# Pacing the gathers of a four-pass graph kernel: seven side sums behind TensorE in place of ten, and in the third pass the product of the gather's own step

## The chip, the cores and the metric

The kernel runs on one core of one Trainium2 chip. The metric is the device time of one execution in microseconds (us); the time that is compared is the median of several executions. Engines are named as in the profile: PE is TensorE, PEld its weight loads, DVE VectorE, ACT ScalarE, POOL GpSimd, SP SyncE. A small q behind a name means the engine's sequencer.

## The reference

Four graph layers over 12,500 nodes of 128 numbers and 200,000 edges that are sorted by their target node. Each layer gathers a source row per edge, scores the edge, takes a softmax over the edges of each target and sums the weighted rows. Layer 0 holds two such passes (its `gatv2_layer` twice), layer 1 is computed by source (a scatter pass), layer 2 has a score that is the sum of one number of the target and one of the source, and layer 3 has eight heads:

```
xj = xl[src];  e = leaky_relu(xj + xr[dst]);  logits = e @ att          # layer 0, twice; layer 3 with 8 heads
score = logit[dst] + logit_src[src]                                    # layer 2: no vector per edge
m = segment_max(logits, dst);  ex = exp(logits - m[dst])
out = segment_sum(ex * xj, dst) / segment_sum(ex, dst)
```

## The kernel before, in words

The edges lie in 1664 steps of 128 (one edge a partition). Sixteen steps make a turn, four steps a chunk, so a pass has 104 turns of four chunks. The function family `sp_edges`, `pool_edges`, `pe_edges`, `act_edges`, `dve_edges` runs one pass, each on its own engine, and is called four times: E0 and E1 (layer 0, source tables gather_a and gather_b), E2 (layer 2, table gather_s, `vector` is False) and E3 (layer 3, table gather_c, eight heads, `wide`). Between E1 and E2 lies a pass of another kind (scatter, lines 1151 to 1340) that the change does not touch. Text below calls E0, E1, E2, E3 the first, second, third and fourth pass.

In one turn, per step g:

- SP loads the turn's tables (L665 to L669), once the sums of the turn four before are all added.
- POOL issues one indirect DMA for each step (L687): it gathers 128 source rows into `rows[:, turn mod 4, g]`. Ahead of it stands a wait, `hold_ge`, on PE's semaphore `side_sums`: ten side sums back. It is a wait for pace alone; that the slot in `rows` is free is told by the wait on `block_sums` four turns back (L684).
- PE makes the side sum of the step (L721 and L722): target row of each edge by a one-hot matmul, plus the gathered source row by a matmul with the identity. For a chunk it waits for the four gathers of that chunk (L711) and for DVE's `larger` two chunks back. In the third pass the side sum is only the target's score (L725, a 128x4 result): it reads no gathered row, and PE does not wait for gathers there.
- ACT and DVE turn the side sums into logits (L862, L908, L915, L921). In the third pass DVE adds the target's score and the source's score once a turn (L1095 to L1103) and waits there for all sixteen gathers of its turn.
- Two turns later PE makes the block sums (L738) from weighted one-hots of ACT (L826) and the gathered rows, and DVE adds them to the totals (L951, L960).
- A chain of small PE transposes (L774, L779, L782, L789, L792) and DVE scans carries the running maxima from turn to turn; DVE's `rescale` (L978) waits for L792, ACT's L826 for the edge distances of PE (L747).

Each engine takes its instructions strictly in program order. `side_sums` is counted by PE as each side sum is finished; `L.side.at(it, k, lag=1)` is side sum k of the turn before.

Of the kernel before, what the change touches and what calls it, by code (L numbers as in the profile page):

```python
# [16 lines left out]
G = 16  # L17
# [1 line left out]
PEEL = 2 * U  # L19
CH = 4  # L20
NCH = G // CH
LEAD = 10
AW = 136
XW = 130
NSUM = 4
# [135 lines left out]
def turns(eng, n, depth, turn, ahead=0):  # L161


    assert ahead <= U
    end = n - U if ahead else n
    for i in range(PEEL):
        turn(Turn(i))
    with eng.Fori(PEEL // U, end // U) as j:
        for u in range(U):
            turn(Turn(u, j))  # L170
    for i in range(end, n + depth):
        turn(Turn(i))


def build(nc, a, out):
# [31 lines left out]
    with ExitStack() as ctx:  # L207
# [468 lines left out]
        def pool_edges(e, L):  # L676
            w = On(e, anchor)
            w.wait_ge(L.opened.at(0))

            def turn(it):  # L680
                u = it.slot()
                w.hold_ge(L.tab.at(it))
                for c in range(NCH):
                    w.hold_ge(L.block.at(it, c, lag=U))  # L684
                    for g in range(c * CH, (c + 1) * CH):
                        w.hold_ge(L.side.at(it, g - LEAD) if g >= LEAD else L.side.at(it, g + G - LEAD, lag=1))
                        e.indirect_dma_start(rows[:, u, g, 0:L.width], None, L.src_rows,  # L687
                                             bass.IndirectOffsetOnAxis(ap=edge_sb[:, u, g:g + 1].bitcast(I32), axis=0)
                                             ).then_inc(L.gat[c].sem(it), 16)
            turns(e, NG, 0, turn)  # L690
# [1786 lines left out]
```

## Time and profile before

| | |
|---|---|
| median of 3 runs | 14911.71 us (14908.64 to 14938.14) |
| the profiled execution, own time | 14998.32 us |
| its span in the trace | 14996.4 us |
| mean granted clock of PE | 0.72 of full speed |
| PE, DVE, ACT, POOL busy | 74%, 53%, 37%, 63% of the span |

Busy shares are averages over stages with different limits. POOL's share counts the time in which it makes a gather's descriptors, not the transfer; what ends an idle stretch is inferred from semaphore events, and "remote" there means that no engine's instruction was found close to the event. "issue" means that nothing in the profile was waited for.

### The profile page before, as it was taken

To read this page: it belongs to the slowest core of one execution; us is meant where nothing else is said; L and a number is where in the kernel's file an instruction comes from. 1 tells how busy PE (TensorE), PEld (TensorE's weight loads), DVE (VectorE), ACT (ScalarE), POOL (GpSimd) and SP (SyncE) were. 2 spreads that over 40 slices of the span, in tenths; PEclk is the share of its full clock that TensorE was granted. 3 is DMA by queue.
4 is the path that set the end of the run, shared out by engine and by line. 5 is a ranking of instruction groups with operands and counts; after the bars stand their busy time and mean duration, and the time that the engine had idled before them with its cause. 6 is when DMAs were issued, how large, how long until landed. Compare 5 with 4: busy or idle time off the path is not lost.

```text
span 14996.4 us, 278163 instructions
## 1 busy us (share of the span) xinstructions
PE 11026.0 (74%) x60653; PEld 8678.6 (58%) x60653; DVE 7973.5 (53%) x29240; ACT 5541.4 (37%) x14105; POOL 9489.8 (63%) x8593
## 2 busy tenths in 40 slices
PE   5777777777777778888888875555555767777776
PEld 4666666666666666666666653344344556666664
DVE  6555555555555555555555553333333566666666
ACT  1444444344444444333333343333333622222223
POOL 3666666466666657888888865566666255655555
PEclk7887788788778775766666765555555877888777
DMA  3111111221111113444444452222222221222222
GB/s 87 45 45 44 44 45 45 88 80 44 45 44 45 44 40 44 39 39 39 39 39 39 39 104 58 44 45 45 45 45 45 60 52 48 50 49 49 50 50 56
DMA packets 808955, 748.01 MB, mean 50 GB/s; under 512 B 264685, under 2 KB 691174, under 8 KB 808254
## 3 DMA queue, kind: packets, MB, share of 16 engines
q0 software_dynamic: 453440, 550.05, 21.1%
q1 hardware_dynamic: 354814, 191.38, 4.9%
q14 instruction: 599, 4.91, 0.1%
q8 instruction: 102, 1.67, 0.0%
HBM read 548.62 MB, written 192.13 MB: 49 GB/s over the span
## 4 chain that ended last, share of the span: by engine, by line
PE 27%; another core or an unknown queue 15%; issue 13%; DMA 9%; DVE 7%; ACT 6%; POOL 2%; SPq 1%; DVEq 1%; ACTq 0%; POOLq 0%
DMA scatter_s<-dst_side 8%; PE bank L738 8%; PE bank L721 3%; PE bank L722 3%; PE bank L1214 3%; ACT oh_e L826 2%; PE bank L1220 2%; PE bank L1229 2%; PE bank L747 2%; PE bank L705 1%; POOL scatter_s L1181 1%; DVE agg L960 1%; DVE lrelu L915 1%; DVE agg L951 1%
## 5 line engine op out<-in xcount | busy, mean ns | idle before, releaser
L738 PE MATMUL bank<-rows,oh_e 128*128 128x130 f32 x9984 | 2172.6, 376 | 1578.7 <-ACT oh_e L826 1172.1
L1181 POOL DMA_INDIRECT scatter_s<-dst_side x1664 | 2568.6, 1544 | 551.9 <-DMA scatter_s<-dst_side 267.1
L738 PEld LDWEIGHTS bank<-rows,oh_e 128*128 128x128 f32 x9984 | 1804.0, 264 | 1918.7 <-issue 1036.4
L826 ACT ACTIVATE oh_e<-bank,weight,minus_w 128x128 f32<-128x128 f32 x4992 | 1880.3, 459 | 2378.4 <-remote 1620.8
L951 DVE SCALAR_TENSOR_TENSOR agg<-agg,rescale,bank 128x130 f32 x4992 | 1683.4, 337 | 1636.6 <-remote 792.6
L722 PE MATMUL bank<-rows,ident 128*128 128x128 f32 x9984 | 2335.9, 319 | 144.8 <-issue 141.1
L687 POOL DMA_INDIRECT rows<-gather_c,edge_sb x1664 | 1650.9, 992 | 1122.4 <-issue 443.9
L687 POOL DMA_INDIRECT rows<-gather_b,edge_sb x1664 | 1672.5, 1005 | 1061.9 <-issue 423.0
L687 POOL DMA_INDIRECT rows<-gather_a,edge_sb x1664 | 1669.1, 1003 | 1008.5 <-issue 412.0
L687 POOL DMA_INDIRECT rows<-gather_s,edge_sb x1664 | 1574.3, 946 | 1061.2 <-issue 443.2
L722 PEld LDWEIGHTS bank<-rows,ident 128*128 128x128 f32 x9984 | 1894.7, 235 | 159.7 <-issue 157.6
L862 ACT ACTIVATE lrelu<-bank 128x512 f32<-128x512 f32 x1248 | 751.2, 602 | 2734.9 <-PE bank L722 1900.8
L721 PE MATMUL bank<-dst_side,oh_t 128*128 x4992 | 1253.8, 338 | 202.5 <-issue 116.5
L721 PE MATMUL bank<-dst_side,hT 128*128 x4992 | 1232.0, 334 | 96.9 <-issue 93.2
L908 DVE TENSOR_TENSOR lrelu<-lrelu,bank 128x512 f32<-128x512 f32 x1248 | 850.5, 681 | 714.4 <-ACT lrelu L862 520.0
L705 PE MATMUL bank<-oh_rows,oh_w 5*128 5x512 bf16 x1664 | 788.6, 474 | 556.5 <-ACT oh_t L811 290.5
L721 PEld LDWEIGHTS bank<-dst_side,oh_t 128*128 128x128 f32 x4992 | 950.9, 236 | 311.4 <-issue 280.7
L721 PEld LDWEIGHTS bank<-dst_side,hT 128*128 128x128 f32 x4992 | 932.2, 232 | 194.5 <-issue 153.8
L1214 PE MATMUL bank<-rows,dst_side 128*128 128x130 f32 x3328 | 775.0, 399 | 343.1 <-DVE dst_side L1290 325.8
L1299 DVE SCALAR_TENSOR_TENSOR dst_side<-iota,edge_sb,bank 128x98 f32<-128x98 f32 x1664 | 432.4, 315 | 1115.9 <-PE bank L1220 1078.3
L738 PE MATMUL bank<-xw,oh_e 128*128 128x136 f32 x3328 | 620.4, 339 | 510.5 <-DVE xw L931 218.2
L1214 PEld LDWEIGHTS bank<-rows,dst_side 128*128 128x128 f32 x3328 | 653.2, 278 | 577.0 <-DVE dst_side L1290 359.6
(352 smaller groups left out, 18169.2 us busy)
## 6 DMA issues: line engine op xcount, KB each, us to landing
rows<-gather_a,edge_sb POOLq DMA_INDIRECT x1664
rows<-gather_b,edge_sb POOLq DMA_INDIRECT x1664
scatter_s<-dst_side POOLq DMA_INDIRECT x1664
rows<-gather_s,edge_sb POOLq DMA_INDIRECT x1664
rows<-gather_c,edge_sb POOLq DMA_INDIRECT x1664
rows<-scatter_s SPq DMA_DIRECT2D x56, 455.0 KB, 6.3
scatter_s<-zeros SPq DMA_DIRECT2D x64, 390.0 KB
edge_sb<-edge_tab SPq DMA_DIRECT2D x520, 40.0 KB
```

What stands on the lines that cost most here:

```text
L687: e.indirect_dma_start(rows[:, u, g, 0:L.width], None, L.src_rows, bass.IndirectOffsetOnAxis(ap=edge_sb[:, u, g:g + 1].bitcast(I32), axis= ...
L705: e.matmul(bank[0][:, :], oh_w[:, :], oh_rows[:, it.slot(lag), c * CH * P:(c + 1) * CH * P], start=True, stop=True).then_inc(L.dist.sem, 1)
L721: e.matmul(o, oh, dst_flat[:, bass.ds(at[g], P)], start=True, stop=False)
L722: e.matmul(o, ident[:, :], rows[:, it.slot(), g, 0:P], start=False, stop=True).then_inc(L.side.sem, 1)
L738: ins = e.matmul(sum_bank(g)[:, (g % 2) * AW:(g % 2) * AW + L.aw], oh_e[:, g % 8, :], r, start=True, stop=True)
L826: e.activation(oh_e[:, g % 8, :], bank[7][:, (g % CH) * P:(g % CH + 1) * P], ACT.Relu, bias=weight[:, it.slot(2, 2), g:g + 1], scale=minus ...
L862: e.mul(lrelu[:, c % 2, :], bank[2 + c % 2][:, :], SLOPE).then_inc(L.sloped.sem, 1)
L908: e.tensor_tensor(lrelu[:, c % 2, :], lrelu[:, c % 2, :], bank[2 + c % 2][:, :], ALU.max).then_inc(L.larger.sem, 1)
L951: e.scalar_tensor_tensor(old, old, rescale[:, it.slot(2, 2), g:g + 1], sum_bank(g)[:, (g % 2) * AW:(g % 2) * AW + L.aw], ALU.mult, ALU.add ...
L1181: e.indirect_dma_start(scatter_s[k], bass.IndirectOffsetOnAxis(ap=S_.target[:, it.slot(1), g:g + 1], axis=0), S_.summed[:, g % 8, :], None ...
L1214: e.matmul(bank[6 + h % 2][:, (g % 2) * XW:(g % 2 + 1) * XW], S_.same[:, g % 8, :], rows[:, v, g, :], start=True, stop=True).then_inc(S_.b ...
L1299: e.scalar_tensor_tensor(S_.scratch[:, g % CH, 0:NB], iota[:, 0:NB], edge_sb[:, u, 4 * G + g:4 * G + g + 1], bank[5][:, (g % CH) * P:(g % ...
```

## The change

The number of side sums that a gather stays behind goes from ten to seven. In the third pass (`L.vector` False) each gather waits for the product of its own turn and step. Nothing else is touched: same instructions, same buffers.

```diff
-LEAD = 10
+LEAD = 7
@@ pool_edges @@
                     for g in range(c * CH, (c + 1) * CH):
-                        w.hold_ge(L.side.at(it, g - LEAD) if g >= LEAD else L.side.at(it, g + G - LEAD, lag=1))
+                        if L.vector:
+                            w.hold_ge(L.side.at(it, g - LEAD) if g >= LEAD else L.side.at(it, g + G - LEAD, lag=1))
+                        else:
+                            w.hold_ge(L.side.at(it, g))
                         e.indirect_dma_start(rows[:, u, g, 0:L.width], None, L.src_rows,
```

On POOL's queue the difference shows where a pass starts, before the wait has a side sum to wait for. The start of the first pass before and after, in POOL's order (side_sums is the semaphore of PE's side sums, x9 that the row stands nine times):

```order
L687 DMA rows<-gather_a,edge_sb 128x128 [waits tables_in_slot0,rows_and_carry_set]
L687 DMA rows<-gather_a,edge_sb 128x128 x9
L687 DMA rows<-gather_a,edge_sb 128x128 [waits side_sums] x6
L687 DMA rows<-gather_a,edge_sb 128x128 [waits side_sums,tables_in_slot1]
L687 DMA rows<-gather_a,edge_sb 128x128 [waits side_sums] x15
```

```order
L690 DMA rows<-gather_a,edge_sb 128x128 [waits tables_in_slot0,rows_and_carry_set]
L690 DMA rows<-gather_a,edge_sb 128x128 x6
L690 DMA rows<-gather_a,edge_sb 128x128 [waits side_sums] x9
L690 DMA rows<-gather_a,edge_sb 128x128 [waits side_sums,tables_in_slot1]
L690 DMA rows<-gather_a,edge_sb 128x128 [waits side_sums] x15
```

Seven gathers go without a wait where ten did; every later gather has moved by three side sums. The start of the third pass on POOL, before and after:

```order
L687 DMA rows<-gather_s,edge_sb 128x129 [waits tables_in_slot0,rows_and_carry_set]
L687 DMA rows<-gather_s,edge_sb 128x129 x9
L687 DMA rows<-gather_s,edge_sb 128x129 [waits side_sums] x6
L687 DMA rows<-gather_s,edge_sb 128x129 [waits side_sums,tables_in_slot1]
L687 DMA rows<-gather_s,edge_sb 128x129 [waits side_sums] x15
```

```order
L690 DMA rows<-gather_s,edge_sb 128x129 [waits side_sums,tables_in_slot0,rows_and_carry_set]
L690 DMA rows<-gather_s,edge_sb 128x129 [waits side_sums] x15
L690 DMA rows<-gather_s,edge_sb 128x129 [waits side_sums,tables_in_slot1]
L690 DMA rows<-gather_s,edge_sb 128x129 [waits side_sums] x15
L690 DMA rows<-gather_s,edge_sb 128x129 [waits side_sums,tables_in_slot2]
```

No gather of the third pass goes without a wait now; each has moved by ten side sums.

## Rows read from the trace of the kernel before

**Rows 1.** The page: the span, and the gathers of the four passes (busy, mean ns, idle)

```profile
span 14996.4 us, 278163 instructions
...
L687 POOL DMA_INDIRECT rows<-gather_c,edge_sb x1664 | 1650.9, 992 | 1122.4 <-issue 443.9
L687 POOL DMA_INDIRECT rows<-gather_b,edge_sb x1664 | 1672.5, 1005 | 1061.9 <-issue 423.0
L687 POOL DMA_INDIRECT rows<-gather_a,edge_sb x1664 | 1669.1, 1003 | 1008.5 <-issue 412.0
L687 POOL DMA_INDIRECT rows<-gather_s,edge_sb x1664 | 1574.3, 946 | 1061.2 <-issue 443.2
```

**Rows 2.** Line 687: ns min/median/max, first to last start; then idle us, times

```profile
L687 POOL DMA_INDIRECT rows<-gather_a,edge_sb x1664: 941/947/1763, 220.7 to 2849.4; - x185
L687 POOL DMA_INDIRECT rows<-gather_b,edge_sb x1664: 941/947/1764, 2952.7 to 5583.7; - x185
L687 POOL DMA_INDIRECT rows<-gather_s,edge_sb x1664: 941/947/1068, 9091.1 to 11698.1; - x185
L687 POOL DMA_INDIRECT rows<-gather_c,edge_sb x1664: 941/947/1796, 12026.2 to 14779.1; - x185
...
  PE bank L722: 1075.5, 687
  remote: 979.3, 536
  PE bank L725: 216.1, 120
```

**Rows 3.** Timeline in the first pass: start, us, engine, line, [idle before]

```profile
1501.86 0.63 PE L722 MATMUL bank<-rows,ident 128*128 128x128 f32 x2
...
1503.28 0.94 POOL L687 DMA_INDIRECT rows<-gather_a,edge_sb  x1 [1.93 <-PE bank L722]
...
1509.90 0.95 POOL L687 DMA_INDIRECT rows<-gather_a,edge_sb  x1 [1.92 <-PE bank L722]
...
1511.72 0.39 PE L722 MATMUL bank<-rows,ident 128*128 128x128 f32 x2
...
1513.65 0.94 POOL L687 DMA_INDIRECT rows<-gather_a,edge_sb  x1 [0.30 <-issue]
...
1515.90 0.60 ACT L862 ACTIVATE lrelu<-bank 128x512 f32<-128x512 f32 x1 [2.38 <-remote]
...
1516.43 0.95 POOL L687 DMA_INDIRECT rows<-gather_a,edge_sb  x1 [1.84 <-PE bank L722]
```

**Rows 4.** Timeline in the third pass

```profile
10001.61 0.95 POOL L687 DMA_INDIRECT rows<-gather_s,edge_sb  x1 [1.79 <-PE bank L725]
...
10007.41 0.17 DVE L1103 TENSOR_TENSOR masked<-logit,edge_sb 128x16 f32<-128x16 f32 x1
...
10011.40 0.28 PE L792 MATMUL bank<-ident,decay_m 16*128 16x16 f32 x1
...
10017.35 0.95 POOL L687 DMA_INDIRECT rows<-gather_s,edge_sb  x1 [0.30 <-issue]
...
10019.21 0.17 DVE L978 TENSOR_SCALAR rescale<-bank 128x16 f32<-128x16 f32 x1 [11.63 <-remote]
```

**Rows 5.** Timeline at the start of the first pass: fourth gather, first side sum

```profile
224.46 0.95 POOL L687 DMA_INDIRECT rows<-gather_a,edge_sb  x1 [0.30 <-issue]
...
227.26 0.79 PE L721 MATMUL bank<-dst_side,oh_t 128*128 x2 [5.23 <-DMA rows<-gather_a,edge_sb]
```

**Rows 6.** Line 721: what PE waited for at it, us and times

```profile
  DMA rows<-gather_c,edge_sb: 36.6, 23
  DMA rows<-gather_b,edge_sb: 16.9, 7
...
  DMA rows<-gather_a,edge_sb: 15.0, 8
```

**Rows 7.** Stretches of the first and third pass: length; busy of PE, PEld, DVE, ACT, POOL; PEclk, DMA share, GB/s

```profile
230.00:2830.00 2600.00, 2010.33 (x12312) 1642.75 (x12311) 1413.53 (x4257) 1072.26 (x2733) 1647.32 (x1643) 0.81 0.18 45
...
9100.00:11690.00 2590.00, 1396.89 (x7401) 1014.23 (x7401) 835.45 (x3354) 861.60 (x2329) 1561.78 (x1651) 0.50 0.21 46
```

## The prediction, made before the changed kernel ran

> **What bounds the kernel now.** The page comes first. Each pass has 1664 gathers [rows 1], and by the view of line 687 the passes run from 220.7 to 2849.4, 2952.7 to 5583.7, 9091.1 to 11698.1 and 12026.2 to 14779.1 us [rows 2]. Over 104 turns that is 25.3, 25.3, 25.1 and 26.5 us a turn. The reader should see how alike these are, though PE is 77% busy in the first pass (2010.33 of 2600 us) and 54% in the third (1396.89 of 2590) at different clocks [rows 7]. What the passes share is POOL: one gather keeps it 1.003 us on average, the next one starts 0.30 us behind it at the earliest [rows 1, 3], so sixteen take 16 x 1.303 = 20.8 us in the first pass, 16 x 1.246 = 19.9 us in the third and 16 x 1.292 = 20.7 us in the fourth. The rest, 4.4, 5.2 and 5.8 us a turn, is time in which POOL waits for side sums. It is in pieces: 687 + 536 + 120 waits of 1075.5 + 979.3 + 216.1 us [rows 2], 3.2 a turn over 416 turns, 1.7 us each or 1.4 us above the 0.30.
>
> The timeline says why a piece is never short. In the first pass a chunk's side sums start to be ready at about 1512.1 (the pair of matmuls that began at 1511.72 took 0.39 us), yet ACT, which needs that chunk, starts at 1515.90, and POOL, which waits for its first sum, at 1516.43 [rows 3]. Between them lies the last gather of a row of four, begun at 1513.65. ACT moved 2.25 us after that start, POOL 2.8 us. The first chunk shown had its first sum finished at 1502.49 while POOL stood still, and POOL went on at 1503.28, 0.8 us later [rows 3]. In the third pass PE is through L792 at 10011.68, DVE's L978, which needs it, starts at 10019.21, 1.9 us after the last of a row of gathers had begun at 10017.35 [rows 4]. So I read: while gathers follow each other without a break, PE's finished work is often not seen by the others until about 2 us after the start of the last gather. A wait of POOL costs 1.9 us (1.93, 1.92 and 1.84) and is also what lets the other engines go on.
>
> Here the Trainium skill speaks against that reading. Its page "SBUF — State Buffer", section "SBUF: two separate sides", says that transfers and engines use disjoint ports and cannot slow each other. The 7.5 us of L978 are not explained by it; by the page alone the distance of the gathers would be mere slack and the sum below would be zero.
>
> **The change, part by part.** No instruction is added: 4 x 1664 gathers keep their 0.95 us and their wait; only the number waited for differs. At the start of the passes fewer gathers go ahead: three less in the first, second and fourth, hidden because PE needs four at first and seven are still free; ten less in the third, once 10 x 1.25 = 12 us at most. I count 12 us.
>
> First, second and fourth pass. After side sum 4c has been seen, gather 4c+7 may start, and it is the last one that the next chunk of side sums needs; before, the fourth gather of a chunk had been released three side sums earlier. The loop from chunk to chunk is: sum seen to gather start 0.8 us [rows 3]; start to landing as PE sees it 2.8 us (224.46 to 227.26) [rows 5]; first sum of the chunk 0.7 to 1.2 us (L721 and L722 pairs, 0.39 to 0.79 us each) [rows 3, 5]. Together at most 4.8 us, less than the 4 x 1.303 = 5.2 us that POOL needs for the four gathers. Two ends follow:
> - every completion is seen at once: POOL never waits, a turn falls to 20.8 us, 4.4 us below today;
> - every chunk's sums are held back until the row of four gathers is over: four waits a turn of 1.93 - 0.30 = 1.63 us, 6.5 us, a turn of 27.3 us, 2.1 us above today.
> Between the ends counts the share h of chunks that are held back: 6.5h against 4.4 us now, so the border is h = 0.68. Now PE can have the sums of two chunks done inside one row of gathers, since its gathers have landed long before (it waited 38 times for one, 68 us in three passes [rows 6]), and one wait then frees eight gathers; with seven it can't. The new first sum of a chunk is finished 2.8 + 0.7 us or more after POOL has gone on. A completion in that position is the one of 1512.1, 2.2 us after POOL went on at 1509.90, and it was held [rows 3]; the one of 1502.49 was free, but POOL stood still there. I take h = 0.8: 5.2 us a turn, +0.8 us. In the fourth pass the waits take 1.4 us more than in the first today (5.8 against 4.4); I leave these and add the same 0.8 us. Behind a waiting gather stand only POOL's other gathers; who waits for them is PE, at the side sums, and behind these in PE's order its block sums, transposes and edge distances.
>
> Third pass. PE's products need no gathered row, so POOL's rhythm stays as it is and only the labels of the gathers move by ten. New is that DVE at L1095 waits for gathers that have just been issued. With chunks two and three released together at about 10001.6, eight gathers start from there on, the last 7 x 1.25 = 8.8 us later at 10010.4, landed at 10013.2 by the 2.8 us of rows 5. L1095 to L1103 take 0.9 us, so the masked scores come at 10014.1 and not at 10007.6. PE transposes them early, but what it hands on is seen at 10019.2 anyway [rows 4]: 5 us of cover, cost nothing. Where a row of gathers ends early the cover is gone and up to 6.5 us would show. I take 0.3 us a turn between 0 and 1.
>
> Sum: 104 x (0.8 + 0.8 + 0.8 + 0.3) + 12 = 293 us. The profiled execution took 14998.32 us for a span of 14996.4 us, 0.6% above the median of the runs shown; I add the 293 us to the median, 14911.71, and get 15,200 us.
>
> **The rivals.**
> - Faster: shorter rows of gathers let completions through. The loop of 4.8 us fits into 5.2 us, and with at most seven ahead the engines behind PE are never cut off as long as in rows 4. It decides from h = 0.68 down. For it speaks that the free loop would take POOL out of its waits altogether; against it the held sum of 1512.1. With h = 0.5 a turn of the three passes is 3.25 - 4.4 = 1.15 us shorter: 3 x 104 x 1.15 = 359 us less, 43 us more for the third pass and the start: 14,600 us.
> - Every chunk is held back (h = 1): 104 x (3 x 2.1 + 0.3) + 12 = 698 us more, 15,610 us. For it: the position of the new first sum late in the row. Against it: some completions do pass.
> - No change: PE's finished work is late for a reason that has nothing to do with how far ahead the gathers are, and the slack of seven is enough, as 38 waits for landings in 312 turns suggest. 14,900 us. The page's rule above would give this.
> - The clock. PE waits more and stays at 1.2 GHz. In the third pass, at 54% busy, the granted clock is 0.50, in the first 0.81 [rows 7]. At 0.50 the 19.5 us of PE in a turn of the first pass would become 31.7 us, above the 25.3 us, and the three passes would lose 6 us a turn, 1900 us: 16,800 us. A PE that is the bound is busy, and it was at 0.81 when busy 77%, so I hold this for improbable. The Trainium skill, "TensorE: Matmul & The Clock Gate", section "HAM oscillation — how this bites in real kernels", describes waits for transfers that bring the clock down; the trace agrees in so far as the pass with the less busy PE has 0.50.
>
> **How the numbers follow.** A measurement of this kernel tells about 0.2% (30 us) from no change. Chances: slower by the partial hold-up 0.42 (15,050 to 15,500 us), every chunk held 0.06, clock 0.02; no change 0.13; faster 0.37 (14,350 to 14,850 us). Slower together 0.50. The range goes from h = 0.43 (2.8 - 4.4 = 1.6 us a turn less in three passes, -456 us: 14,450) to h = 1 (15,600); about 0.1 is left out below and 0.06 above. The forecast's own range, without the faster case, is 15,050 to 15,600.
>
> **What the changed profile would show.** If right: POOL's waits for PE L722 more in number, near four a turn, still 1.8 to 1.9 us each, few rows of gathers longer than four; PE waiting for rows<-gather at L721 hundreds of times in place of 38; turns of 26 us in the first two passes; the third pass at 25 us a turn with DVE waiting at L1095 for rows<-gather_s. If the rival is right: fewer or shorter waits of POOL, the turn below 25 us, and in the third pass L978 no longer 7 us behind L792. The prediction is wrong if the share of held-back chunks falls with shorter rows of gathers, or if the order of the third pass, where DVE now waits, changes which completions meet a row of gathers.

## The result and the profile after

| | us | ratio to before (95% interval) |
|---|---|---|
| before, median of 6 | 14907.83 | |
| changed, median of 6 | 14976.85 | 1.0041 (1.0030 to 1.0053) |
| changed, profiled execution: span | 14967.4 | |

The kernel became 0.41% slower (the ratio), some 62 us; the two medians lie 69 us apart. The forecast was 15,200 us, some 290 us slower.

The page of the changed kernel, the rows that answer to [rows 1]:

```profile
span 14967.4 us, 278163 instructions
...
L690 POOL DMA_INDIRECT rows<-gather_c,edge_sb x1664 | 1661.3, 998 | 1075.2 <-PE bank L725 501.3
L690 POOL DMA_INDIRECT rows<-gather_b,edge_sb x1664 | 1660.6, 998 | 1060.9 <-PE bank L725 444.0
L690 POOL DMA_INDIRECT rows<-gather_a,edge_sb x1664 | 1661.3, 998 | 997.8 <-PE bank L725 416.8
L690 POOL DMA_INDIRECT rows<-gather_s,edge_sb x1664 | 1574.5, 946 | 1105.5 <-issue 448.7
```

The view of its gather line, as [rows 2] (L690 is L687 of before; L725 and L728 are L722 and L725):

```profile
L690 POOL DMA_INDIRECT rows<-gather_a,edge_sb x1664: 942/947/1764, 220.4 to 2830.3; - x185
L690 POOL DMA_INDIRECT rows<-gather_b,edge_sb x1664: 942/947/1761, 2932.4 to 5551.8; - x185
L690 POOL DMA_INDIRECT rows<-gather_s,edge_sb x1664: 942/947/1083, 9064.1 to 11712.2; - x185
L690 POOL DMA_INDIRECT rows<-gather_c,edge_sb x1664: 942/947/1800, 12033.7 to 14750.2; - x185
...
  PE bank L725: 1362.2, 893
  remote: 599.2, 367
  PE bank L728: 341.9, 122
```

The waits rose from 1343 to 1382, but the mean wait fell from 1.69 to 1.67 us. The spans of the two first profiles mislead: before's own is 0.6% above its median, so the changed kernel looks faster there. They can't be subtracted; hence a second profile of before, below.

What PE waited for at line 724, as [rows 6], and DVE at line 1098 (L1095 of before), which waited there once, for 7.9 us:

```profile
  DMA rows<-gather_c,edge_sb: 199.0, 134
  DMA rows<-gather_b,edge_sb: 69.8, 39
  DMA rows<-gather_a,edge_sb: 46.4, 23
```

```profile
L1098 DVE TENSOR_REDUCE logit<-bank x104: 219/225/226, 9085.6 to 11717.2; 128x16 f32<-128x64 f32 x104
its engine sat idle before it (us, times) until:
  DMA rows<-gather_s,edge_sb: 124.2, 38
```

PE now waits 196 times for a landing in place of 38, 315 us in place of 68, and DVE 38 times, 3.3 us each. Both are as the forecast described them, in kind. For PE these named waits are the smaller part: the row "issue" of the same view, idle time for which the profile names no cause, rose from 644.2 to 1913.4 us. The timeline of the changed kernel in the first pass:

```profile
1515.07 0.95 POOL L690 DMA_INDIRECT rows<-gather_a,edge_sb  x1 [0.30 <-issue]
...
1515.33 0.39 PE L725 MATMUL bank<-rows,ident 128*128 128x128 f32 x2
...
1518.32 0.94 POOL L690 DMA_INDIRECT rows<-gather_a,edge_sb  x1 [2.31 <-PE bank L725]
...
1518.90 0.61 ACT L865 ACTIVATE lrelu<-bank 128x512 f32<-128x512 f32 x1
```

The pair that holds the first sum is over at 1515.72, yet POOL goes on 2.6 us later, 3.25 us after the last gather of the row began. The delay that the forecast was built on is there.

Of the signs that the forecast named, some are there and some are not. Landings at line 724 are waited for hundreds of times. But POOL waits 3.3 times a turn (1382 over 416 turns) and not near four, the first two passes take 25.1 and 25.2 us a turn and not 26, and the third 25.5.

### The profile page after: what moved, and what is told of

Its sections match the earlier page's. It is cut to its first block, busy times and chain, and to the rows that moved or that the text cites. A ratio compares the mean times of both kernels' runs of the same rounds, so it can differ in the third digit from the quotient of the medians.

```text
span 14967.4 us, 278163 instructions
## 1 busy us (share of the span) xinstructions
PE 11047.6 (74%) x60653; PEld 8764.4 (59%) x60653; DVE 7967.3 (53%) x29240; ACT 5571.8 (37%) x14105; POOL 9480.8 (63%) x8593
## 3 DMA queue, kind: packets, MB, share of 16 engines
q8 instruction: 102, 1.67, 0.0%
## 4 chain that ended last, share of the span: by engine, by line
PE 31%; another core or an unknown queue 14%; issue 11%; DMA 8%; DVE 8%; ACT 5%; POOL 2%; DVEq 1%; ACTq 0%; POOLq 0%; SPq 0%
PE bank L741 7%; DMA scatter_s<-dst_side 6%; PE bank L724 4%; PE bank L725 4%; PE bank L1217 3%; PE bank L1223 2%; ACT oh_e L829 2%; PE bank L1232 2%; PE bank L750 2%; PE bank L708 1%; DVE agg L963 1%; DVE lrelu L918 1%; POOL scatter_s L1184 1%; DMA rows<-gather_c,edge_sb 1%
## 5 line engine op out<-in xcount | busy, mean ns | idle before, releaser
L741 PE MATMUL bank<-rows,oh_e 128*128 128x130 f32 x9984 | 2076.0, 364 | 1006.0 <-ACT oh_e L829 615.5
L741 PEld LDWEIGHTS bank<-rows,oh_e 128*128 128x128 f32 x9984 | 1734.6, 256 | 1335.1 <-issue 681.9
L725 PE MATMUL bank<-rows,ident 128*128 128x128 f32 x9984 | 2424.2, 333 | 1.1 <-issue 0.7
L690 POOL DMA_INDIRECT rows<-gather_c,edge_sb x1664 | 1661.3, 998 | 1075.2 <-PE bank L725 501.3
L690 POOL DMA_INDIRECT rows<-gather_b,edge_sb x1664 | 1660.6, 998 | 1060.9 <-PE bank L725 444.0
L690 POOL DMA_INDIRECT rows<-gather_a,edge_sb x1664 | 1661.3, 998 | 997.8 <-PE bank L725 416.8
L690 POOL DMA_INDIRECT rows<-gather_s,edge_sb x1664 | 1574.5, 946 | 1105.5 <-issue 448.7
L725 PEld LDWEIGHTS bank<-rows,ident 128*128 128x128 f32 x9984 | 2005.5, 249 | 2.0 <-issue 1.9
L724 PE MATMUL bank<-dst_side,oh_t 128*128 x4992 | 1319.8, 356 | 522.9 <-issue 306.7
L724 PE MATMUL bank<-dst_side,hT 128*128 x4992 | 1265.0, 343 | 526.2 <-issue 386.9
L724 PEld LDWEIGHTS bank<-dst_side,oh_t 128*128 128x128 f32 x4992 | 1017.1, 253 | 627.8 <-issue 614.2
L724 PEld LDWEIGHTS bank<-dst_side,hT 128*128 128x128 f32 x4992 | 969.2, 241 | 625.3 <-issue 605.6
L1071 DVE TENSOR_TENSOR shifted<-masked,bank 128x16 f32<-128x16 f32 (+1 forms) x416 | 83.3, 200 | 1654.3 <-remote 1170.5
```

Source lines behind the costliest of these rows:

```text
L724: e.matmul(o, oh, dst_flat[:, bass.ds(at[g], P)], start=True, stop=False)
L725: e.matmul(o, ident[:, :], rows[:, it.slot(), g, 0:P], start=False, stop=True).then_inc(L.side.sem, 1)
L741: ins = e.matmul(sum_bank(g)[:, (g % 2) * AW:(g % 2) * AW + L.aw], oh_e[:, g % 8, :], r, start=True, stop=True)
```

## The experiments

All runs are compared with the kernel before, run beside them on the same chip. That matters here. The 18 runs were made in five groups, and before took 14909, 14979 and 14983 us in three of the groups and 12863 and 12864 us in the two others. I call these the first and the second kind of chip. It was not chosen which one a group got, and whether the chip or something around it differs is not known: the record gives a number for the chip, and number 9 stands both with a group of the second kind (e4 to e7) and with one of the first kind (e8 to e10).

| run | back, vector passes / third | kind | ratio (95% interval) |
|---|---|---|---|
| e0_before | 10 / 10 | first | 1.0003 (0.9993 to 1.0013) |
| e1_vector7 | 7 / 10 | first | 1.0033 (1.0022 to 1.0044) |
| e2_third_own | 10 / own step | first | 1.0015 (1.0006 to 1.0024) |
| e8_after_again, e15_after | 7 / own step | first | 1.0047 (1.0033 to 1.0062), 1.0044 (1.0030 to 1.0058) |
| e3_vector4_third7 | 4 / 7 | first | 1.1809 (1.1793 to 1.1826) |
| e17_lead13 | 13 / 13 | first | 1.0320 (1.0298 to 1.0341) |
| e10_no_pace_again | no wait | first | 1.2186 (1.2166 to 1.2207) |
| e9_break | 10 / 10, break after each gather | first | 1.2374 (1.2354 to 1.2393) |
| e16_break_no_pace | no wait, break after each fourth | first | 1.0585 (1.0524 to 1.0646) |
| e4_lead13, e11_lead13_again | 13 / 13 | second | 1.0005 (0.9996 to 1.0014), 1.0001 (0.9991 to 1.0010) |
| e5_no_pace | no wait | second | 0.9996 (0.9987 to 1.0005) |
| e6_pad | 10 / 10, six idle waits after each gather | second | 1.0009 (1.0000 to 1.0018) |
| e7_third7 | 10 / 7 | second | 1.0005 (0.9996 to 1.0014) |
| e14_vector6 | 6 / 10 | second | 1.0610 (1.0592 to 1.0628) |
| e12_break_no_pace | no wait, break after each fourth | second | 1.1184 (1.1165 to 1.1203) |
| e13_chunk_break | 10 / 10, break after each fourth | second | 1.1412 (1.1393 to 1.1432) |

### The change in its two parts

e0_before is the kernel before, unedited. The others change only the numbers:

```diff
-w.hold_ge(L.side.at(it, g - LEAD) if g >= LEAD else L.side.at(it, g + G - LEAD, lag=1))
+if L.vector:   # e1: 7, e2: 10, e3: 4
+    w.hold_ge(L.side.at(it, g - 7) if g >= 7 else L.side.at(it, g + G - 7, lag=1))
+else:          # e1: 10, e2: L.side.at(it, g), e3: 7
+    w.hold_ge(L.side.at(it, g - 10) if g >= 10 else L.side.at(it, g + G - 10, lag=1))
```

> The kernel before, unchanged, for a second profile of it. Its first profile took 14998 us where its runs have a median of 14908, and the changed kernel's profile took 14969 us where its runs have a median of 14977; so the lengths of the passes in those two profiles can't be set against each other yet. Ratio 1.000. If the excess of 90 us in the first profile was chance, the four passes are here shorter together by some 90 us: I expect it in the three passes with vectors (2629, 2631 and 2753 us there), since POOL's pauses are the part of a turn that is not fixed. If it sits outside the four passes, the pass lengths of the first profile can be used as they are.

> Only the first part of the change: seven back in the first, second and fourth pass, ten back in the third. Theory of the prediction (completions of PE are held back while gathers follow each other; share h of chunks held): the measured 62 us of the whole change, less what the third pass costs (2648 against 2607 us in the two profiles, 41 us), leave some 20 us for three passes, h about 0.69: ratio 1.001 to 1.002. Rival (what the two profiles say as they are: 19, 12 and 36 us less in the three passes): ratio 0.996. Second rival (all the loss is here, the third pass is neutral as the prediction had it): 1.004.

> Only the second part: ten back in the first, second and fourth pass, the product of the own step in the third. By the profiles +41 us, ratio 1.0028. By the prediction (0.3 us a turn and 12 us at the start) +43 us, 1.003: the two agree, so this run can only speak against both. Rival (the third pass carries more than the whole loss, the other passes gain): +60 to +130 us, 1.004 to 1.009, and the pass by itself more than 2660 us long.

> Four back in the first, second and fourth pass, seven back in the third. With four, gather 4c+4 waits for the first sum of chunk c, so the next chunk's gathers start only when this chunk's sums are seen: the loop of a chunk is 0.8 us + three gathers 3.9 us + landing 2.8 us + first sum 0.7 to 1.2 us = 8.2 to 8.7 us, four times a turn is 33 to 35 us, each of the three passes some 800 us longer: ratio about 1.16. If landings and first sum are faster than these rows say, 1.10. Third pass at seven: theory that only the labels of the gathers move there: within 10 us of the pass of before (2607 us). Rival (shorter rows of gathers let completions through): shorter by 50 us or more.

The second profile of before:

```profile
L687 POOL DMA_INDIRECT rows<-gather_a,edge_sb x1664: 938/944/1762, 221.1 to 2818.7; - x185
L687 POOL DMA_INDIRECT rows<-gather_b,edge_sb x1664: 938/944/1764, 2920.8 to 5514.2; - x185
L687 POOL DMA_INDIRECT rows<-gather_s,edge_sb x1664: 938/944/1067, 9021.7 to 11659.3; - x185
L687 POOL DMA_INDIRECT rows<-gather_c,edge_sb x1664: 938/944/1823, 11987.9 to 14719.0; - x185
```

The passes are 2598, 2593, 2638 and 2731 us long, against 2629, 2631, 2607 and 2753 us in [rows 2]: three shorter, as expected, and the third longer. So one profile of this kernel gives the length of a pass only to about 30 us. Only the timed ratios can carry a difference of 60 us, and they do: the first part costs 0.33% (49 us), the second 0.15% (22 us), together 71 us beside the 62 us of the whole. Of the rivals for e1 the gain falls. The other, that all of the loss is in this part (1.004), lies inside the interval of e1 (1.0022 to 1.0044); what speaks against it is e2, whose interval (1.0006 to 1.0024) leaves out 1. The main expectation for e1, 1.001 to 1.002, was too low, and the 1.0028 for e2 too high. e3 hit the first pass: four back makes 33.8 us a turn (3510.6 us for 104), 8.4 us a chunk where 8.2 to 8.7 had been put together from rows, and the second and fourth pass are 3535 and 3563 us long. The ratio 1.18 is above the 1.16 expected, since the turns before were 24.9 to 26.3 us long in these passes and the loss is nearer 900 than 800 us a pass. Its third pass, seven back, took 2606 us, within the expected 10 us of 2607; but at ten back three profiles have 2607, 2638 and 2615 us, so this says little.

### Is PE's finished work held back?

> The wait for a side sum is taken out of the gathers altogether; a gather is held only by its buffer (block sums of the turn four before). If PE's completions are held back while gathers follow each other, rows of sixteen gathers and more appear, the other engines stand meanwhile, and the turn is sixteen gathers (20.8 us) and then the work that was cut off: over 28 us a turn, ratio 1.08 or more. Rival (nothing is held back, the pace is idle time of POOL that something else sets): the pauses move to the wait for the block sums and the turn stays at 25 us, ratio 0.99 to 1.01.

> The kernel before with six waits on a semaphore that was reached long ago behind each gather, so that POOL's queue has a short break after each of them in place of 0.30 us; all other waits as before. I expect 0.3 to 0.4 us more between gathers, 16 x 1.6 = 25.5 us a turn without any pause. Theory of held completions, if a break of 0.7 us is enough to let them through: POOL's long pauses all but vanish, L978 is no longer seven us behind L792 in the third pass, turn 25.5 to 26 us, ratio 1.00 to 1.03. If only a break of about 2 us after a gather lets them through: the pauses stay and the padding is added, 16 x 0.35 = 5.6 us a turn, ratio 1.14. Rival (the turn is set by a loop that has nothing to do with POOL): the padding disappears in the pauses, ratio 1.00, with PE, DVE and ACT idle as before.

> Thirteen side sums back in all four passes (buffers allow up to sixteen). Theory of held completions: rows of gathers grow, fewer waits but longer ones, and engines behind PE are cut off longer; with ten a pass has 2.6 waits of over 1 us a turn and 4.3 us of pause a turn, with seven 2.8 and 4.4 us. If the sum of pauses is what the other engines need, it stays: within 0.3 us a turn, ratio 0.993 to 1.007. Rival (POOL's pauses are a cost of waiting closely): each three sums further back save as much as from seven to ten, 0.33%: ratio 0.997 or less.

> Ten back in the first, second and fourth pass, seven in the third. In the run with four in the vector passes and seven in the third the third pass was 2606 us long; with ten it was 2607, 2638 and 2615 us in three profiles, with the own step 2647 and 2648 us. If only labels move there, ratio 1.000 (within 0.001). If the own step's cost is that DVE waits for gathers just issued, seven lies between ten and own step (zero), near ten: 1.000 to 1.0005. Rival (a gain of 15 us or more by seven): 0.999 or less.

These four fell on the second kind of chip. In none of them did the time move by more than 0.2%, and the reason stands in their profiles. Line 690 of e7_third7, whose vector passes are those of before, and its first and third pass in busy times (columns as in [rows 7]):

```profile
L690 POOL DMA_INDIRECT rows<-gather_a,edge_sb x1664: 940/944/1757, 217.6 to 2335.6; - x185
...
L690 POOL DMA_INDIRECT rows<-gather_s,edge_sb x1664: 940/944/1096, 8081.8 to 10159.2; - x185
...
  issue: 1428.8, 4684
  PE bank L725: 538.5, 1766
```

```profile
230.00:2330.00 2100.00, 1698.98 (x12392) 1414.67 (x12391) 1417.85 (x4289) 1110.21 (x2755) 1597.54 (x1649) 0.94 0.22 55
9300.00:9700.00 400.00, 279.23 (x1460) 201.79 (x1460) 164.02 (x660) 169.38 (x460) 302.46 (x321) 0.50 0.26 57
```

The third pass takes 2077.4 us for 1663 steps from gather to gather, 1.249 us each: POOL never stops, and the 1766 waits for PE (of all four passes) are 0.30 us each, which is the gap between any two gathers. The turn is 20.0 us, what the forecast had as the floor of this pass (19.9). Here POOL is the bound and the distance to the side sums is free; the granted clock in the first pass is 0.94 in place of 0.81. On this kind the forecast's second end ("every completion is seen at once") is simply the case, at ten back as well. e6_pad broke no row: its gathers kept their 0.30 us, so the six waits added nothing between them. What it was meant to show it could not.

The no-wait kernel and a real break behind each gather were then run on the first kind:

```diff
+pad = sb("pad", [P, 64]);  self.breaks = each("gather_breaks")
 ...).then_inc(L.gat[c].sem(it), 16)
+e.memset(pad[:, :], 0.0).then_inc(L.breaks.sem, 1)
+w.hold_ge(L.breaks.at(it, g))
```

> The changed kernel once more. The kernel before took 14909 us beside the runs with seven and four back and 12863 us beside the runs with thirteen back and with no pace: two chips of different behaviour. In the profiles of the second there is no pause of POOL at all (every gather 0.30 us behind the one before, 20.0 us a turn in the third pass), so on such a chip the distance can't matter: ratio 0.999 to 1.002, of which 12 us at the start of the third pass would be 0.0009. On a chip as the first one: 1.0041 again, between 1.003 and 1.005.

> The kernel before (ten back), and behind each gather a small memset of POOL for whose end POOL waits, so that the next gather can't start 0.30 us behind; the six waits of the padded run were hidden in the gather before (its gathers kept 0.30 us), so that run broke no row. I expect about 0.3 to 0.5 us more between gathers. On a chip without pauses: 16 x 0.4 = 6.4 us a turn on top of 20.0 to 20.9, four passes 2400 us longer less what PE's own time (19.5 us busy) leaves, ratio 1.15 to 1.22. On a chip as the first one, theory (PE's completions are held while gathers follow within 0.3 us, and pass when there is a real break): the long pauses vanish, turn 16 x 1.65 = 26.4 us against 25.1, ratio 1.02 to 1.05. If a longer silence is needed: pauses stay and the breaks are added, ratio over 1.12.

> No wait for a side sum at all, once more. On a chip without pauses the same as before (0.9996 there). On a chip as the first one, theory of held completions: rows of gathers run on until a buffer is missing, the engines behind PE are cut off for whole rows: ratio 1.03 or more, with fewer and much longer pauses of POOL and many slow steps of SP's sequencer. Rival (the sum of the pauses is set by something else, for example by what PE needs, and only moves from wait to wait): 0.995 to 1.01.

The same kernel without pace is 0.9996 on one kind and 1.2186 on the other. Its timeline on the first kind, first pass:

```profile
1502.21 1.17 PE L737 MATMUL bank<-rows,oh_e 128*128 128x130 f32 x8
1502.69 0.33 DVE L950 SCALAR_TENSOR_TENSOR agg<-agg,rescale,bank 128x130 f32 x1
...
1507.83 0.39 PE L720 MATMUL bank<-dst_side,hT 128*128 x2 [0.93 <-issue]
...
1509.95 0.37 PE L721 MATMUL bank<-rows,ident 128*128 128x128 f32 x1 [1.62 <-issue]
...
1512.08 0.60 PE L721 MATMUL bank<-rows,ident 128*128 128x128 f32 x2 [1.32 <-issue]
...
1512.83 0.60 ACT L861 ACTIVATE lrelu<-bank 128x512 f32<-128x512 f32 x1 [9.99 <-PE bank L721]
...
1516.71 0.94 POOL L686 DMA_INDIRECT rows<-gather_a,edge_sb  x1 [0.30 <-issue]
1520.84 0.35 DVE L950 SCALAR_TENSOR_TENSOR agg<-agg,rescale,bank 128x130 f32 x1 [17.82 <-remote]
...
1531.88 1.03 POOL L686 DMA_INDIRECT rows<-gather_a,edge_sb  x1 [14.23 <-DMA step_sb<-step_tab]
```

Gathers run on without a gap until 1516.71. DVE stands for 17.82 us, though the block sums that it needs were over at 1503.38; then everything behind PE moves within 11 us while POOL stands for 14.23 us. Two things are seen here. The word of PE's finished work comes late (DVE), and PE itself is slow: the four side sums of one chunk, between which the program has no wait, take from 1503.65 to 1512.68, with gaps of up to 1.62 us for which the profile names no cause. ACT's 9.99 us are of this second sort, since PE's last side sum was over only 0.15 us before. Over the first pass such gaps of more than 0.3 us inside a chunk's side sums come to 310 us (370 of them) without the wait, to 72 and 48 us in the two profiles of before, to 0.4 us in the changed kernel and to none in e5, e7 and e9. I counted them from the kept traces.

The hand-over from PE to DVE that took 7.5 us in [rows 4] can be quick. At one place in the third pass of e9_break, where POOL stands, and on the second kind at one where the gathers follow without a gap (e7_third7):

```profile
11505.40 0.28 PE L796 MATMUL bank<-ident,decay_m 16*128 16x16 f32 x1
11506.05 0.17 DVE L982 TENSOR_SCALAR rescale<-bank 128x16 f32<-128x16 f32 x1 [1.09 <-PE bank L796]
```

```profile
9303.48 0.94 POOL L690 DMA_INDIRECT rows<-gather_s,edge_sb  x1 [0.30 <-issue]
9303.80 0.28 PE L795 MATMUL bank<-ident,decay_m 16*128 16x16 f32 x1
9304.45 0.17 DVE L981 TENSOR_SCALAR rescale<-bank 128x16 f32<-128x16 f32 x1 [1.10 <-PE bank L795]
```

It is 0.37 us from the end of the matmul to DVE in both. Single places prove little, so here is the same wait of DVE over the third pass, from the view of its line: 909 us for 101 of them in the first profile of before and 370 us for 101 in the second; 163 us for 102 in e9_break, on the first kind but with breaks; 130 us for 102 in e5 and e7, on the second kind.

The kept traces hold one thing more that bears on the whole pass: the times at which each semaphore was raised. Beside the end of each side sum of the first pass (its first and last turns left out) I set the first raising of `side_sums` that is not more than 0.06 us earlier. A raising that belongs to the side sum before can be taken for it, so the lateness is put rather too low. Between 0.3% and 12% of the raisings are missing from a trace, so differences of a few per cent say nothing.

| run | back | kind | raised over 0.5 us late | over 1.5 us late | median, us |
|---|---|---|---|---|---|
| e3_vector4_third7 | 4 | first | 5% | 4% | 0.01 |
| e1_vector7, changed kernel, e8, e15 | 7 | first | 59% to 62% | 32% to 36% | 0.87 to 0.93 |
| before, e0_before, e2_third_own | 10 | first | 62% to 65% | 39% to 46% | 1.04 to 1.27 |
| e17_lead13 | 13 | first | 66% | 50% | 1.52 |
| e10_no_pace_again | none | first | 42% | 29% | 0.01 |
| e16_break_no_pace | none, break after each fourth | first | 56% | 32% | 0.69 |
| e9_break | 10, break after each | first | 7% | 3% | 0.01 |
| all eight of the second kind | 6, 10, 13, none | second | at most 1.2% | at most 1% | 0.01 |

In [rows 3] the four side sums that end between 1512.11 and 1513.45 are raised in one burst between 1515.66 and 1515.88; ACT starts at 1515.90 and POOL's next gather at 1516.43. So it is shown that on the first kind the others get word of PE's work late when gathers follow each other within 0.3 us, and that it comes in time when there is a break after every gather (0.88 to 1.2 us between them in the timeline), or on the second kind. It is not DVE alone that is held: in [rows 3] it is ACT and POOL. What the lateness costs by itself is not shown. The 22% of the no-wait kernel are made of both, of it and of PE's own gaps.

The break was dearer than expected: gathers follow each other at 2.0 us in the timeline and at 2.1 to 2.2 us on the average of a pass, in place of 1.25. So e9_break is slower, 1.24 against the 1.02 to 1.05 expected. By its number it lies with the other branch (over 1.12, "a longer silence is needed"), but the table speaks against the reason given there: the raisings are in time.

### Where the loss per step back lies

> Six back in the first, second and fourth pass, ten in the third. Loop of a chunk with six back: sum seen to gather start 0.8 us, one more gather 1.3, landing 2.8, first sum 0.7 to 1.2: 5.6 to 6.1 us, four times 22.4 to 24.4 us, below the turn of 25.2: by the loop alone the same as seven back, 1.003. If the pause after each row adds to the loop (a completion is seen only when the row is over), four pauses a turn of 1.63 us on 20.8: 27.3 us, three passes 2.1 us a turn more, 1.044. What comes out between them is the share of chunks that are held. (By the same loop four back was 8.2 to 8.7 us; measured 33.8 us a turn, 8.4 a chunk.)

> No wait for side sums; in its place a small memset behind every fourth gather, for whose end POOL waits, 1.05 us between two gathers there in place of 0.30 (as in the run with a break behind each gather). Theory: a break of this length is enough for PE's completions to pass, so rows are never longer than four (4.0 us of gathers and a break): 16 x 1.303 + 4 x 0.75 = 23.8 us a turn in the first pass against 25.0 to 25.3, ratio 0.94 to 0.98 if no other pause is left, against 1.2186 without breaks. Rival (the others need POOL to wait for them, a blind break helps only by chance): 1.05 or more. On the other kind of chip (before at 12860 us) the breaks only cost: 3 us a turn less what PE takes anyway, 1.04 to 1.09.

> Breaks as in e12, and the pace of ten back kept. Theory: as e12 but with what is left of the pauses of POOL added where it runs ahead: 0.95 to 0.99, L978 close behind L792 in the third pass. If breaks and pauses add up (4 x 0.75 = 3.0 us a turn, four passes): 1.08. On the other kind of chip: 1.04 to 1.09.

> Thirteen side sums back in all passes, on a chip where before takes some 14950 us. If longer rows of gathers cost because more completions meet them, thirteen lies on the way from ten (1.000) to no pace at all (1.2186): 1.02 to 1.08, with rows of up to twelve gathers more often and longer pauses. Rival (the sum of pauses is conserved as between seven and ten): 0.997 to 1.003. On a chip where before takes 12860 us: 1.000.

In e12 and e13 the breaks stand once a chunk (the two lines of e9_break one level further out). All four fell on the second kind. e14_vector6, first pass:

```profile
L690 POOL DMA_INDIRECT rows<-gather_a,edge_sb x1664: 938/944/1641, 217.9 to 2567.2; - x185
```

That is 22.6 us a turn, 5.65 us a chunk: the bare loop, free of held completions, inside the 5.6 to 6.1 us of the rows. Seven back would be one gather of 1.25 us less, 4.4 us, and fit under the 5.2 us of POOL, as the prediction said; that is an estimate, for seven back in the vector passes never ran on the second kind. The time missed both expectations (1.003 and 1.044): they took the turn of the first kind, and against the 20.4 us here 22.6 is a loss. e12 and e13 show only what breaks cost where nothing is held, 1.118 and 1.141 where 1.04 to 1.09 was expected. Last, on the first kind:

> The changed kernel. On the chip where before takes 12863 us: the loop of a chunk at six back was 5.65 us in the first pass there (2349 us for 104 turns of four chunks), at seven back it is a gather of 1.25 us shorter, 4.4 us, below the 5.0 to 5.2 us that four gathers take: no pause, 1.000; the start of the third pass adds up to 12 us, 1.0009. On a chip as the first: 1.003 to 1.005 a third time.

> No wait for side sums and a break of POOL behind every fourth gather (1.18 to 1.12 times the time of before was measured on the other chip, where it only costs: 24.1 us a turn). On a chip as the first one, theory that a break of 1 us in place of 0.30 lets PE's completions pass: the turn is the same 24.1 us as on the other chip, against 25.1 to 26.2, so a time near 14400 us: ratio 0.96. If such a break is too short or four gathers in a row already too long: between 1.00 and 1.22.

> Thirteen back in all passes. On a chip as the first one: if longer rows cost, 1.02 to 1.08 on the way to 1.2186 without pace; if the sum of pauses is conserved, 0.997 to 1.003. On the other kind of chip 1.000 a third time.

Of the distances tried ten is thus the best there: 1.181 at four, 1.003 at seven (both in the vector passes), 1 at ten, 1.032 at thirteen, 1.219 without a wait. Thirteen loses most in the fourth pass, 3004.5 us in e17_lead13 against 2731 us in e0_before.

e16 brings the no-wait kernel from 1.2186 to 1.0585, so breaks help, but one after every fourth gather does not replace the wait. The expectation of 0.96 failed, and 56% of the raisings in the table are still late. The same break was long enough in e9_break, after every gather, so a row of four gathers is the likelier reason; no run tells the two apart. Its POOL still stood 217 times, for 1701.4 us or 7.8 us each, at the turn's tables.

POOL's row for 320 to 2500 us of the first pass, at ten back (e0_before), seven (changed kernel) and thirteen (e17_lead13):

```profile
L687 POOL DMA_INDIRECT rows<-gather_a,edge_sb x1391 | 1385.8, 996 | 794.4 <-issue 341.0 <-PE bank L722 257.4 <-remote 174.2
```

```profile
L690 POOL DMA_INDIRECT rows<-gather_a,edge_sb x1386 | 1381.6, 997 | 798.9 <-PE bank L725 359.2 <-issue 343.6 <-remote 72.2
```

```profile
L687 POOL DMA_INDIRECT rows<-gather_a,edge_sb x1360 | 1355.6, 997 | 825.8 <-issue 422.4 <-PE bank L722 251.4 <-remote 148.3
```

Idle less 0.30 us a gather, over count / 16 turns: (794.4 - 417.3) / 86.9 = 4.34 us of pause a turn, (798.9 - 415.8) / 86.6 = 4.42, and (825.8 - 408.0) / 85.0 = 4.92. In the same stretch the view of the line counts 198 + 94 waits for side sums in e0_before and 254 + 52 in the changed kernel:

```profile
  PE bank L722: 257.4, 198
  remote: 174.2, 94
```

```profile
  PE bank L725: 359.2, 254
...
  remote: 72.2, 52
```

3.36 a turn of 1.48 us became 3.53 a turn of 1.41 us: above the 0.30, 3.96 us and 3.92 us a turn. More waits, each shorter, and almost the same sum. The three profiles were not taken side by side, and other profiles put a measure on that: the other two with seven back and both parts (e8, e15) have 3.56 and 3.44 waits of 1.21 and 1.22 us above the 0.30, and the first of before has 3.10 of 1.34 us. e1_vector7, which was run beside e0_before, has a pause of 4.46 us a turn, of it 3.82 us in 3.34 waits for side sums. So its loss of 0.16 us a turn (49 us over 312 turns) is not in those waits; the rest of POOL's idle time grew there, from 0.38 to 0.64 us a turn. Why is not shown.

## Why the prediction was wrong

- **What bounds the kernel: right.** POOL's gathers and its pauses set the turn on the first kind; without pauses the turn is 20.0 to 20.4 us. The reading of held completions was drawn from two or three places in the trace, so it was lucky to hold as widely as the table of raisings shows. By the prediction's reading of the Trainium skill's page "SBUF — State Buffer", section "SBUF: two separate sides", the distance would have been slack everywhere. The second kind agrees (0.9996 without a wait); the first does not (1.2186), and there the measurement decides. What the runs contradict is that reading and not the page's sentence, which is on ports: no run here shows transfers and engines contending for one.
- **The loop from chunk to chunk: right.** 8.4 us at four back, 5.65 at six.
- **"I take h = 0.8: 5.2 us a turn, +0.8 us": mis-sized, and the step that failed.** 104 x 0.8 x 3 = 250 us was forecast, 49 us measured (0.33%). I priced a held chunk with one whole pause of 1.63 us and set the product against today's 4.4 us. The number was not far off (3.2 waits a turn forecast, 3.53 counted), the price was: 1.11 us above the 0.30 (1.11 to 1.22 in three profiles). Today's waits were already 3.36 a turn at 1.18 us, so the same count that I forecast stood in the rows of before (3.2 a turn in my own first paragraph, 1.4 us each), and no rise could follow from it. The pauses of 1.84 to 1.93 us that I took for the price are the long ones. With seven back the word is late almost as often as with ten (59 to 62% of the side sums against 62 to 65%), but by less: the median lateness is 0.87 to 0.93 us in place of 1.04 to 1.27.
- **Where h came from.** The held side sum of 1512.1 was finished 2.2 us after POOL had gone on. The new first sum was reckoned at 3.5 us or more, so "a completion in that position" did not have that position, and h = 0.8 rested on one place.
- **The third pass: kind right, size half.** +43 us forecast, +22 us measured (9 to 36). DVE does wait for gathers just issued, 124 us in all, 1.2 us a turn, four times what I took. It costs little since the lateness of L978 behind it is not what sets the pass: between 9300 and 11500 us L978's idle time before it falls from 815.3 us for 88 of them in the first profile of before to 305.0 for 87 in the second, while the pass was 2607 us in the first and 2638 in the second. Nor are 12 us lost at the start that any run shows.
- **The rivals.** "Shorter rows let completions through" is true in one way: waits got shorter, and in the third pass of the changed kernel DVE waits 2.5 us each time at L978's place and not 7 us, as that rival said (but 3.5 us already in the second profile of before). It balanced the greater number and gained nothing. The clock did not move (0.80 and 0.81 in the first pass). "No change" was the nearest of the values named, 14,900 us, but the measured difference is clear of zero. The direction that came out had been given a chance of one half.
- What stays open: the ends of matmuls are modelled in a profile, so a late raising can't be told from a matmul that truly ended late; what it is in a row of gathers that holds the word and, in long rows, PE itself; and in what the two kinds of chip differ. Why ten is the best of the distances tried is not shown: lateness grows from four to thirteen back (the table) and the loop from chunk to chunk grows the other way, which fits, but no run changes the length of a row alone.

## What to carry to other kernels

When a forecast multiplies a count of waits by a price, run the same product on the kernel before first: if it does not give today's sum, the price is wrong. A wait that is there for pace alone is tuned to a machine, so compare it only beside the old value on the same chip: here thirteen and no wait at all are free on one and cost 3% and 22% on another. A mechanism read from two or three places of a timeline should be counted over a whole pass before it is priced. Differences under half a per cent come from timed ratios, not from the lengths of passes in single profiles.

## What the hardware showed that I had not expected

The same kernel took 14909 to 14983 us in three groups of runs and 12863 us in two, 14% less, nearly all of it in the four passes with gathers (2593 to 2731 us against 2077 to 2170 us; e7_third7 has ten back in three of them). On the first kind six in ten raisings of PE's semaphore came over 0.5 us after the end of the matmul, on the second hardly one in a hundred. A small memset and a wait for it between two gathers of POOL raise their distance from 1.25 to 2.0 us or more, though the memset is 0.17 us long; six waits for a semaphore reached long ago, put in the same place, cost nothing that can be told from zero (1.0009, 1.0000 to 1.0018, on the second kind).
